# A two-layer graph network on one core: a first sweep of 46 steps with ten counted tiles each, and five groups of the edge network ahead of it

## What is computed

```
# layer 0: a graph convolution
deg  = segment_sum(1, src)                       # how often a node is a source
norm = rsqrt(deg)[src] * rsqrt(deg)[dst]
x = layernorm(x + segment_sum(norm * (x @ W)[src], dst) + b)
# layer 1: messages weighted by a network of the edge features
w_ij  = silu(rad @ rw0 + rb0) @ rw1 + rb1 + silu(sph @ sw0 + sb0) @ sw1 + sb1
q, k, v = (x @ wq)[dst], (x @ wk)[src], (x @ wv)[src]
alpha = sum over 16 of (q * w_ij * k), per head, times edge_weight
x = layernorm(x + segment_sum(alpha * v, dst))
```

## Time and profile before

| | |
|---|---|
| time, median of 3 (lowest, highest) | 1765.84 us (1764.24, 1766.24) |
| the profiled execution: own time, span | 1775.31 us, 1773.5 us |
| mean granted clock of TensorE | 0.978 |
| busy PE, DVE, POOL, ACT | 89%, 78%, 74%, 52% |
| first sweep, from layer 1 of step 0 to the last window | 94.94 to 620.93 us |

### The profile page before, as it was taken

How to read it: one execution, slowest core, us unless ns; L and a number is a source line. 1 busy time by engine, 2 the same in 40 slices (tenths; PEclk the granted TensorE clock), 3 DMA queues, 4 the chain that set the end, 5 groups by cost and what they waited for, 6 DMA issues and landing times.

```text
span 1773.5 us, 45704 instructions
## 1 busy us (share of the span) xinstructions
PE 1572.9 (89%) x12986; PEld 1456.7 (82%) x12986; DVE 1379.2 (78%) x3866; ACT 926.0 (52%) x1399; POOL 1310.4 (74%) x1252
## 2 busy tenths in 40 slices
PE   3389999899899977999999999999999999999995
PEld 2278888888888865999999988988888988889884
DVE  8886777777777455888887878778887888878786
ACT  1144555555555365666555555555555555555563
POOL 7877777777777637777777777777777777777771
PEclk9999999999999987999999999999999999999997
DMA  3133333333333247766666666666666666666663
GB/s 100 43 106 101 107 104 99 108 102 99 107 104 106 72 145 190 192 175 177 174 176 181 175 180 174 171 174 175 177 178 176 172 173 173 176 176 173 182 171 104
DMA packets 177657, 259.26 MB, mean 146 GB/s; under 512 B 80694, under 2 KB 91757, under 8 KB 177436
## 3 DMA queue, kind: packets, MB, share of 16 engines
q0 software_dynamic: 51840, 132.72, 28.1%
q1 hardware_dynamic: 120008, 120.99, 24.3%
q10 hardware_dynamic: 5716, 4.55, 0.9%
HBM read 235.32 MB, written 22.79 MB: 146 GB/s over the span
## 4 chain that ended last, share of the span: by engine, by line
POOL 44%; issue 18%; PE 15%; DVE 14%; DVEq 4%; DMA 2%; POOLq 1%; ACTq 1%; SPq 1%; ACT 1%
POOL arena L667 40%; PE bank L961 5%; PE bank L1004 4%; DVE count L1351 4%; POOL rel L622 3%; DVE xsplit L1318 2%; DVE key_hot L1339 2%; DVE low_hot L1338 2%; PE bank L971 2%; DVEq L1324 1%; PE bank L943 1%; DVEq L1351 1%; POOLq L684 1%; DMA arena<-kv_d,idx 1%; DMA xraw<-in_sph_t 1%
## 5 line engine op out<-in xcount | busy, mean ns | idle before, releaser
L667 POOL DMA_INDIRECT arena<-kv_d,idx x808 | 833.1, 1031 | 260.4 <-issue 257.3
L961 PEld LDWEIGHTS bank<-w,hid 128*128 128x128 f32 x6464 | 783.6, 194 | 24.3 <-issue 1.7
L961 PE MATMUL bank<-w,hid 128*128 128x128 f32 x6464 | 792.3, 278 | 0.0
L784 ACT ACTIVATE hid<-bank,b 128x512 f32<-128x512 f32 x808 | 496.1, 682 | 321.9 <-PE bank L945 302.8
L667 POOL DMA_INDIRECT arena<-xs_d,idx x408 | 394.3, 966 | 136.9 <-issue 121.3
L943 PE MATMUL bank<-xsplit,w_hi 128*128 128x512 f32 x808 | 344.8, 437 | 73.3 <-ACT hid L784 49.8
L776 ACT ACTIVATE xsplit<-xraw 64x1024 fp32r<-64x1024 f32 x202 | 212.3, 1052 | 218.7 <-DMA xraw<-in_sph_t 206.8
L1318 DVE TENSOR_TENSOR xsplit<-xraw,xsplit 64x256 fp32r<-64x256 f32 x808 | 287.6, 412 | 6.4
L943 PEld LDWEIGHTS bank<-xsplit,w_hi 128*128 128x128 f32 x808 | 154.8, 192 | 105.3 <-ACT hid L784 56.7
L1351 DVE TENSOR_TENSOR count<-count,bank 128x200 f32 x400 | 144.9, 362 | 123.8 <-issue 57.4
L971 PE MATMUL bank<-onehot,late 128*128 128x126 f32 x1616 | 216.5, 283 | 6.6 <-DVE late L1534 5.6
(11 more groups left out here) (144 smaller groups left out, 1306.4 us busy)
## 6 DMA issues: line engine op xcount, KB each, us to landing
late<-relrow_d SPq DMA_DIRECT2D x103, 256.0 KB
xraw<-in_rad_t SPq DMA_DIRECT2D x205, 128.0 KB
xraw<-in_sph_t SPq DMA_DIRECT2D x410, 64.0 KB
w_sb<-w_d SPq DMA_DIRECT2D x52, 256.0 KB
w_d<-w_sb SPq DMA_DIRECT2D x51, 256.0 KB
arena<-kv_d,idx POOLq DMA_INDIRECT x808
arena<-xs_d,idx POOLq DMA_INDIRECT x408
qwin<-q_d SPq DMA_DIRECT2D x101, 31.5 KB
```

Of the source, the lines that this page charges most:

```text
L667: pool.indirect_dma_start(gath[:, k, t * width:(t + 1) * width], None, table, bass.IndirectOffsetOnAxis(ap=idx[:, pair.slot(4), j * TILES ...
L784: act.activation(hid[:, s.slot(2), c, :], hid_ps[s.sub(4, c, 4 * s.total).slot(len(hid_ps))][:, :], ACT.Silu, bias=b0[:, c:c + 1]).then_in ...
L961: mm = pe.matmul(w_ps[:, t * D:(t + 1) * D], hid[:, b, c, t * P:(t + 1) * P], w1[:, c, :], start=False, stop=(c == 3), skip_group_check=True)
```

## The change

- The first sweep has `UNITS1` = 46 steps; 368 tiles are gathered and `DENSE` = 440 are counted, ten in each of 44 steps, in five batches (`BATCHES`). The last two steps count nothing. There are 12 span sums for 13, over windows of 176 columns for 144 (`WIDE`).
- `hots` builds the one-hots of two tiles with one instruction each (a compare of two tensors, 128x256 and 128x400 elements), from digits stored twice (`low2`, `key2`).
- On PE layer 2 is cut in two halves with a batch between them; on DVE batch 3 stands ahead of the window, and batch 4 behind it.
- Five groups of the edge network are computed ahead (`layer1_ahead`, `layer2_ahead`, `silu_ahead`, `keep_ahead`), in plain fp32 for layer 1 instead of the split: 14 of the 16 chunks of the first two between steps of the degree count, the rest of them and layer 1 of the third behind it, and 8 chunks of layer 1 and 12 of layer 2 behind the flag's matmul. Their stores are issued by ACT; the stores of `xs` move from ACT to SP.

```diff
-UNROLL1, LAST1 = 8, 8
+UNROLL1, LAST1 = 8, 3
-WIDE = 144
+WIDE = 176
-BATCHES = 4
+BATCHES = 5
+DENSE_TILES = 2 * BATCHES
+AHEAD = 5
...
+    UNITS1 = UNITS - AHEAD
+    SPANS = UNITS1 // SPAN + 1
+    COLS1 = UNITS1 * 2 * TILES
...
+            def silu_ahead(r):
+                for c in range(4):
+                    act.wait_ge(mlp0.s_l1, 4 * r + c + 1)
+                    if c == 0 and r >= 2:
+                        act.wait_ge(mlp0.s_w, r - 1)
+                    act.activation(hid[:, r % 2, c, :], ahead_ps[c][:, :], ACT.Silu, bias=b0[:, c:c + 1]).then_inc(mlp0.s_silu, 1)
+            def keep_ahead(r):
+                act.wait_ge(mlp0.s_w, r + 1)
...
+                act.activation(w_sb[:, r % 2, :], bank[7][:, :], ACT.Copy).then_inc(s_wcopy0, 1)
+                act.wait_ge(s_wcopy0, r + 1)
+                act.dma_start(w_d[(UNITS1 + r) * P:(UNITS1 + r + 1) * P, :], w_sb[:, r % 2, :]).then_inc(s_wstore0[r % 2], 16)
+            silu_ahead(0)
+            silu_ahead(1)
+            keep_ahead(0)
             act.wait_ge(s_pre, PRE.deg)
...
+            silu_ahead(2)
...
+            for r in range(3, AHEAD):
+                keep_ahead(r - 2)
+                silu_ahead(r)
+            for r in range(AHEAD - 2, AHEAD):
+                keep_ahead(r)
             act.wait_ge(s_pre, PRE.passes)
...
+            def layer1_ahead(r, c):
...
+                if r >= 1:
+                    pe.wait_ge(mlp0.s_silu, 4 * (r - 1) + c + 1)
+                pe.matmul(ahead_ps[c][:, :], w0_raw[rows, m, cols], xraw[rows, k, m, :],
+                          start=True, stop=True).then_inc(mlp0.s_l1, 1)
+            def layer2_ahead(r, c):
+                pe.wait_ge(mlp0.s_silu, 4 * r + c + 1)
+                if c == 0:
+                    if r >= 1:
+                        pe.wait_ge(s_wcopy0, r)
+                    pe.matmul(bank[7][:, :], ones[0:2, :], b1_wide, start=True, stop=False, skip_group_check=True)
+                for t in range(TILES):
+                    mm = pe.matmul(bank[7][:, t * D:(t + 1) * D], hid[:, r % 2, c, t * P:(t + 1) * P], w1[:, c, :],
+                                   start=False, stop=(c == 3), skip_group_check=True)
...
+            for c in range(DEG_LOOP, DEG_STEPS):
+                count_src(Step(c, total=DEG_STEPS))
+                turn, place = divmod(c - DEG_LOOP, 3)
+                if place < 2 and turn < 7:
+                    first_two(2 * turn + place)
+            first_two(14)
+            first_two(15)
+            for c in range(4):
+                layer1_ahead(2, c)
...
             pe.matmul(bank[0][:, 0:1], ones[:, :], small[:, 2:3], start=True, stop=True).then_inc(s_viol, 1)
+            for r in range(3, AHEAD + 1):
+                for c in range(4):
+                    if r < AHEAD:
+                        layer1_ahead(r, c)
+                for c in range(4):
+                    layer2_ahead(r - 1, c)
...
-                layer2(s, mlp1, w1_ps[0])
+                layer2(s, mlp1, w1_ps[0], range(2))
                 if dense:
                     count_batch(s, 2)
+                layer2(s, mlp1, w1_ps[0], range(2, 4))
+                if dense:
+                    count_batch(s, 3)
                 sum1(s)
                 if dense:
-                    count_batch(s, 3)
+                    count_batch(s, 4)
...
-                for t in range(2 * j, 2 * j + 2):
-                    col = s.sub(2 * TILES, t, DENSE).n
-                    dve.tensor_scalar(low_hot[:, t, :], iota_key[:, 0:LO], low_f[:, ds(col, 1)], None, ALU.is_equal)
-                    last = dve.tensor_scalar(key_hot[:, t, :], iota_key[:, :], key[:, ds(col, 1)], None, ALU.is_equal)
+                first = s.sub(DENSE_TILES, 2 * j, DENSE).n
+                for hot, digit, w in ((low_hot, low2, LO), (key_hot, key2, KEYS)):
+                    shape = [P, 2, w // 2, 2]
+                    values = iota_key[:, 0:w].rearrange("p (a k) -> p a k", k=2).unsqueeze(1).to_broadcast(shape)
+                    last = dve.tensor_tensor(hot[:, 2 * j:2 * j + 2, :].rearrange("p t (a k) -> p t a k", k=2),
+                                             digit[:, ds(first, 2), :].unsqueeze(2).to_broadcast(shape), values,
+                                             ALU.is_equal)
```

More of the change, by code:

```diff
@@ L186, in build @@
         xraw = sb("xraw", [RAD, 3, 2, GE])
+        with ExitStack() as below:
+            dig = below.enter_context(nc.sbuf_tensor("dig", [P, 2, DEG_STEPS * DEG_COLS, 2], BF16))
         xsplit = sb("xsplit", [P, 2, 2, GE], F32R)
@@ L471, in sweep1 @@
                 load_idx(s, s_idx1, s_gath1, 4)
+                if s.before(2):
+                    last = max(r for r in range(AHEAD) if ahead_slots[r] == s.c)
+                    sp.wait_ge(mlp0.s_l1, 4 * last + 4)
                 load_features(s, mlp1, s.sub(4, 0, G))
@@ L799, in sweep1 @@
                 act.wait_ge(mlp1.s_w, s.tick + 1)
-                if not s.before(2):
+                if s.before(2):
+                    act.wait_ge(s_wstore0[s.c], 16 * ((AHEAD + 1 - s.c) // 2))
+                else:
                     act.wait_ge(s_wstore[s.slot(2)], ((s - 2).round(2) + 1) * 16)
@@ L1373, in sweep1 @@
                 batch(1)
-                if more:
+                if not s.is_last(2):
                     split_lo(s + 2, mlp1)
```

124 lines of the change are left out of this document (82 added, 42 removed).

## The result

The changed kernel takes 1810.51 us (median of four runs, 1808.11 to 1813.77) where the kernel before took 1766.04 on the same chip: 1.0248 of it, 95% interval 1.0217 to 1.0278, 44.5 us slower. I had forecast 1762.5 and a range up to 1776. The profiled execution took 1808.18 (span 1806.4), near its median. Against the profiled 1775.31 of before that is 32.9 us, but up to the end of the first sweep the two traces differ by 42.1 (last window at 663.07, before 620.93); behind it the profiled run of before was the slower one, by 9.3, which is how far it lay above its median. So all of the loss lies ahead of the end of sweep 1, 32.6 us of it ahead of the first split layer 1.

What follows compares the result with a forecast made beforehand. It took DVE's pace to bound three steps of four, with PE's span sum added in the fourth (41.3 us a cycle). The sweep's -20.4 us and +17.1 ahead of it gave -3.3: 1762.5 us, range 1744 to 1776.

Steps and rivals of the forecast that it cites:

- One-hots, 0.48 us a batch for 0.69: In DVE's sweep batches: two two-tile compares, 0.20 + 0.28 us, replace four small ones taking 0.69 us.
- + 0.08 (ten offsets for eight; the load of eight is 0.60): In a DVE step's last batch: loading ten offsets instead of eight adds 0.08 us.
- Forecast for the sweep 505.6 us: Whole first sweep: 32.2 us start, ten cycles 439, end 34.4; 505.6 for 526.0, 20.4 us gained.
- the two legs on TensorE: PE's part of a four-step cycle: span sum 7.58 us, half of layer 2 1.79, then 3.96 to batch 4's start.
- head and tail: Sweep ends: 32.2 us from first layer 1 to first span sum, 34.4 us after the ten cycles.
- I cost this at nothing: Chunks beside the degree count: PE falls some 3 to 5 us behind, covered by DVE's ring and a wait; cost nothing.
- My second rival: Ahead work holds up the degree count: chunks of 1.8 us at slow pace, count ending 75 or later, 1773.5; chance 0.18.
- I add 1.9 for that: Groups ahead behind the flag: PE starts slow after idling, adding 1.9 us to 21.5 us of work.
- my 112: Start of the sweep: first split layer 1 at 112 us for 94.94, 17 us lost.
- -20.4 + 17.1 = -3.3: Whole kernel: 20.4 us gained in the sweep, 17.1 lost ahead of it, net -3.3 us.
- GpSimd as a floor of 40.5 a cycle: Sweep gathers on POOL: eight at 1.27 us a step, 40.5 us for four steps, taken as only a floor.
- My first rival: Cheaper DVE steps: a batch's one-hots take 0.34 us, cycle 42.0, 20 us less, 1743; chance 0.20.

Runs made afterwards that it cites:

- experiment 4: The kernel before with two-tile one-hots alone (8 tiles, 51 steps, nothing computed ahead); 1771.4 us (1.0021).
- experiment 1: The changed kernel with its offset row laid out 16 places a step, ten used, so every load starts at a multiple of 64 bytes; 1793.56 us (1.0146).
- experiment 15: The changed kernel with offset rows of 16, eight offsets loaded at a step's head and two behind the feature split; 1784.85 us (1.0087).
- 8: The changed kernel with offset rows of 16; first two groups' layer-1 chunks read other operands filling 128 rows, so their weights are wrong; 1797.13 us (1.0154).
- 11: The kernel of 8 with GpSimd held behind its long subtraction until the degree count ended; 2450.28 us (0.9842), when every kernel took 1.4 times as long.
- 2: The changed kernel with its offset row laid out 12 places a step, starts at multiples of 48 bytes; 1792.54 us (1.0152).
- 7: The changed kernel with offset rows of 16, chunks ahead beginning behind step 9 of the degree count instead of step 21, one every second step; 1800.64 us (1.0187).
- 16: The changed kernel with rows of 16, eight and two offsets, layer 1 ahead on 128 rows, chunks from step 9, GpSimd's short operations held; 1767.88 us (1.0001).
- 17: The kernel of 16 with the load of the fifth group's features put ahead of the `xs` stores on SP's queue; 1760.27 us (0.9933).
- 6: The changed kernel with offset rows of 16 and all five groups computed behind the degree count and flag, none beside the count; 1815.3 us (1.0258).
- 18: The kernel of 17 without holding GpSimd, so its short operations run beside the degree count again; 1761.66 us (0.9956).
- 10: The kernel before with its eight offsets loaded by pairs between adds and one-hots; 2527.95 us (1.0155), when every kernel took 1.4 times as long.
- 3: The kernel before with its eight offsets in rows of ten places a step, so odd steps load from 8 bytes beside a multiple of 16; 1789.38 us (1.0122).
- 14: The kernel of 11 repeated on another chip; 2456.93 us (0.987), when every kernel took 1.4 times as long.

## Why the prediction was wrong

- **One-hots, 0.48 us a batch for 0.69: right.** Adds and one-hots of a batch take 1.25 (mine 1.26). The two compares last 289 and 362 ns by form, but overlap: from start to start they take 0.20 and 0.27 us (experiment 4).
- **"+ 0.08 (ten offsets for eight; the load of eight is 0.60)": this step failed, and it is the sweep's whole miss.** I scaled a row by the count. A load of ten from a multiple of 16 bytes takes 1.07, 0.47 more; one from 8 bytes beside it 2.30. Forecast for the sweep 505.6 us, measured 535.6; with the starts mended 521.2 (experiment 1), with eight at the head as well 506.9 (experiment 15). So 14.4 us were the start of the odd loads, 14.3 the length of all, and 1.3 is left for everything else: the two legs on TensorE (the span sum took 7.48 for 7.58), head and tail were right.
- **"I cost this at nothing" (chunks in the degree count): failed.** The flag came 8.7 us late (91.26 for 82.56). My second rival had this mechanism and its test (the count's end past 75), with too short a chunk (1.8, measured 2.07) and chance 0.18. It held that TensorE "would then be busy without a break" against itself. It was busy, and stayed at half pace for 30 us. As TensorE never waited there, this alone set the end of its count. Behind it stood a second limit that I had not seen: GpSimd's subtraction ends 1.4 us after VectorE first pauses, and its short operations then stretch VectorE's one-hots from 764 to 1304 ns. It shows once the pace is mended: full pace in 8 brings back 1.6 us of the count's end (82.77 to 81.21), full pace without the short operations 11.6 (71.15 in 11). A run without the short operations at half pace was not made.
- **"I add 1.9 for that" (slow pace behind the flag): mis-sized.** Layer 1 of group 3 took 7.48 for 3.9, the bias matmul 1.91 for 1.1, the two next layers 2 took 5.98 and 5.47 for 3.84: 8.2 in all, with the granted clock at 0.50 from 90 to 104 and 0.56 to 0.58 from 112 to 116. With it the first layer 1 follows the flag by 36.2 us, not by 29.4. This and the 8.7 are the 15.5 by which 127.49 misses my 112.
- **Sum.** Forecast -20.4 + 17.1 = -3.3; measured 9.6 + 32.55 = 42.1 in the traces. Of the 45.5 between, 30.0 are the sweep and 15.5 the start.
- **GpSimd as a floor of 40.5 a cycle** was read too lightly: I saw a margin of 1 us a cycle in it, and experiment 4 shows that there is none: with gathers of 0.99 us for 0.96 the floor itself is 41.3, and a VectorE made 3.6 us freer gained nothing. My first rival, cheaper steps of VectorE, could not have paid in full either.

I had put the 2.07 us at 69.89 down to a TensorE that had idled. But a TensorE without a break took 2.07 us a chunk as well, from 43.59 on, where the chunks filled 64 and 32 rows (the kernel after), and 1.13 from 49.29 where they filled 128 (8). How GpSimd and VectorE hold each other up no run shows; measured are the 1304 ns for 764, and a subtraction that ended 1.4 us behind VectorE's first pause.

What stays open is what made the granted clock fall to 0.50. It was there in the kernel after from 90 to 104 us, in 1, 2 and 15 much the same, in 7 from 86 to 108, in 8 from 64 to 72 and again from 88 to 102, in 16 from 86 to 94, in 17 from 94 to 96. Transfers alone don't do it: the DMA share was 0.03 at most where the clock fell in 7 (84 to 88) and 0.00 where it fell in 8 (62 to 66), and in 6 the clock stood at 1.00 beside a share of 0.94. In each of these cases TensorE had run at full pace before, and then waited in part (7, from 81; 8, from 52; 16, from 81.4; 17, 0.83 us at 91) or went over to matmuls of 64 and 32 rows (the kernel after, from 84.64); no run takes the two apart. Why the small profiled differences behind the first sweep are there (up to 12 us between 17 and 18) was not looked into.

## What to carry to other kernels

Before more work goes into a step, look at the sequencer's loads in the chain: how many values each takes and where it starts are a cost at the step's head (0.60 to 2.30 us here). Here rows of 16 places, which put every start at a multiple of 64 bytes, took the load of ten in odd steps from 2.30 us to 1.07, and rows of 12 (48 bytes) did the same (1.06 to 1.08). Work put into an engine's gaps is free only if the engine runs there at the pace you costed it with; price it at half pace until a row shows full pace for that very shape (2.07 us a chunk for 1.16 in the kernel after). Look also at what else waits for such a gap: here GpSimd's long subtraction ended 1.4 us behind a short pause of VectorE (at 48.9 us in the kernel after), and its next work ran beside one-hots of 1304 ns for 764. And take a saving on the engine in the chain only down to the next floor: here it stood less than 1 us a cycle below.

## What the runs showed of the hardware

- Loads into VectorE's registers: one value 0.31 us (a base), two 0.53 (10), and, from starts at multiples of 16 bytes, eight 0.60 and ten 1.07; eight from 8 bytes beside such a start 1.86 (3), ten 2.30 (the kernel after).
- TensorE at half pace (2.07 us a chunk) through 30 us without a break, with the granted clock at 1.00 (43.59 to 73): chunks of 64 and 32 rows between the count's matmuls until 65.3, of 128 rows from 68.42 (the kernel after). At full pace (1.13) from 49.29 where matmuls of 128 rows stood in the same places (8; in 16 from 40.8). In 6 the same: half pace from 85.02 on 64 and 32 rows (14.89 us for eight matmuls), full pace from 107.85 (3.89 for four), behind matmuls of 128 rows.
- GpSimd's subtraction of 808 columns took 51 us beside a VectorE that never paused in the count (before; 50.54 in 14), 29.67 when VectorE paused at 48.9 (the kernel after) and 14.45 when it paused at 33.2 (17): in the last two it ended 1.4 us behind the first pause.
- VectorE's one-hots of 1152 elements beside GpSimd's short operations: 1304 ns for 764 (the kernel after); from 34.6 to 44.3 us, 1123 beside them (18) and 796 with GpSimd held (17).
